# New tokens' value projection in half units between the units of the first attention batches, its product added to the turned attended rows

## The reference

```python
q = jnp.einsum('bsd,ed->bse', x, wq)            # x is the layer norm of the input
k_new = jnp.einsum('bsd,ed->bse', x, wk)
v_new = jnp.einsum('bsd,ed->bse', x, wv)
k = jnp.concatenate([k_cache, k_new], axis=1)   # k_cache = v_cache = the context, 1601 rows
v = jnp.concatenate([v_cache, v_new], axis=1)
scores = jnp.einsum('bqd,bkd->bqk', q, k) * scale
attn = jax.nn.softmax(scores, axis=-1)
out = jnp.einsum('bqk,bkd->bqd', attn, v)       # then out @ wo
```

## Time and profile before

| | |
|---|---|
| median of 3 runs | 1305.7 us (1304.93 to 1308.2) |
| the profiled execution | 1310.41 us |
| its span in the trace | 1308.3 us |
| PE busy | 93% of the span |
| DVE busy, ACT busy | 63%, 48% of the span |
| mean granted TensorE clock | 0.97 |

### The profile page before, as it was taken

How to read it: one execution, slowest core, us unless ns; L and a number is a source line. 1 busy time by engine, 2 the same in 40 slices (tenths; PEclk the granted TensorE clock), 3 DMA queues, 4 the chain that set the end, 5 groups by cost and what they waited for, 6 DMA issues and landing times.

```text
span 1308.3 us, 18916 instructions
## 1 busy us (share of the span) xinstructions
PE 1214.6 (93%) x7634; PEld 1046.4 (80%) x7634; DVE 829.7 (63%) x1013; ACT 628.3 (48%) x562; POOL 97.2 (7%) x82
## 2 busy tenths in 40 slices
PE   4999989888998899999999399999999999999995
PEld 3888766666766688888888398989999999999894
DVE  7332479999999746645546465656556565656464
ACT  4111279888888733113543244444454445454430
POOL 0000100000000000000000011212111111111101
PEclk9999989999998799999999599999999999999998
DMA  7235299999999763421233356676766766676632
GB/s 297 92 129 193 73 360 359 347 388 368 366 356 380 278 267 131 159 97 65 81 123 129 127 184 213 213 213 202 228 212 203 214 218 207 219 209 222 192 128 32
DMA packets 68053, 277.14 MB, mean 212 GB/s; under 512 B 22456, under 2 KB 22600, under 8 KB 45344
## 3 DMA queue, kind: packets, MB, share of 16 engines
q1 hardware_dynamic: 57312, 245.58, 52.3%
q0 software_dynamic: 10688, 30.81, 9.2%
HBM read 258.02 MB, written 18.35 MB: 211 GB/s over the span
## 4 chain that ended last, share of the span: by engine, by line
PE 72%; DVE 13%; DMA 8%; issue 3%; ACT 2%; POOL 0%; SPq 0%; ACTq 0%; DVEq 0%; POOLq 0%
PE ps L1291 22%; PE ps L1292 21%; PE ps L1293 21%; DVE lo L810 10%; DMA out<-y,target 2%; PE ps L1455 2%; DMA raw_more<-new_values 2%; ACT hi L554 1%; PE ps L1387 1%; PE ps L1677 1%; DMA raw<-context 1%; DMA raw<-new_values 1%; DVE scores L888 1%; DMA raw<-keys 1%; PE ps L1406 1%
## 5 line engine op out<-in xcount | busy, mean ns | idle before, releaser
L810 DVE TENSOR_TENSOR lo<-raw,hi 128x2048 fp32r<-128x2048 f32 (+1 forms) x204 | 458.0, 2258 | 173.7 <-ACT hi L554 171.4
L554 ACT ACTIVATE hi<-raw 128x2048 fp32r<-128x2048 f32 (+1 forms) x204 | 383.3, 1888 | 292.8 <-PE ps L1293 270.7
L1291 PE MATMUL ps<-act_hi,hi 128*128 128x240 f32 (+1 forms) x1152 | 333.3, 289 | 9.9 <-DVE act_lo L833 4.8
L1293 PE MATMUL ps<-act_hi,lo 128*128 128x240 f32 (+1 forms) x1152 | 334.2, 290 | 0.0
L1292 PE MATMUL ps<-act_hi,hi 128*128 128x240 f32 x1024 | 283.1, 276 | 0.0
L1291 PEld LDWEIGHTS ps<-act_hi,hi 128*128 128x128 f32 x1152 | 219.0, 190 | 17.7 <-DVE act_lo L833 5.2
L1293 PEld LDWEIGHTS ps<-act_hi,lo 128*128 128x128 f32 x1152 | 219.6, 191 | 5.2
L1292 PEld LDWEIGHTS ps<-act_hi,hi 128*128 128x128 f32 x1024 | 193.8, 189 | 0.3
L1291 PE MATMUL ps<-hi,act_hi 128*128 128x512 f32 x384 | 151.2, 394 | 0.0
L1293 PE MATMUL ps<-hi,act_lo 128*128 128x512 f32 x384 | 149.7, 390 | 0.0
L1292 PE MATMUL ps<-lo,act_hi 128*128 128x512 f32 x384 | 149.5, 389 | 0.0
(11 more groups left out here) (204 smaller groups left out, 1348.0 us busy)
## 6 DMA issues: line engine op xcount, KB each, us to landing
raw<-weights SPq DMA_DIRECT2D x128, 1024.0 KB, 4.9
raw<-keys SPq DMA_DIRECT2D x32, 1024.0 KB, 10.1
raw<-context SPq DMA_DIRECT2D x32, 1024.0 KB, 9.4
raw_more<-keys SPq DMA_DIRECT2D x16, 1024.0 KB, 10.3
raw_more<-context SPq DMA_DIRECT2D x16, 1024.0 KB, 9.7
xq<-x_in SPq DMA_DIRECT2D x4, 512.0 KB, 6.5
new_keys_t<-kvs POOLq DMA_DIRECT2D x8, 256.0 KB, 3.1
new_values<-kvs POOLq DMA_DIRECT2D x8, 256.0 KB, 2.3
```

Of the source, the lines that this page charges most:

```text
L554: act.activation(part(hi, k, kind), part(raw, k, kind), ACT.Copy).then_inc(hi_done, 1)
L810: dve.tensor_tensor(part(lo, k, kind), part(raw, k, kind), part(hi, k, kind), ALU.subtract).then_inc(lo_done, 1)
L1291: pe.matmul(out, a_hi, b_hi, start=first, stop=False)
L1293: return pe.matmul(out, a_lo, b_hi, start=False, stop=last)
```

## The change

The value projection is no longer a stage of its own. Its four units become 8 half units ("block", 128 x 1024), each of which gives 128 dimensions of the new values for all 512 tokens, turned (`value_block`, 24 matmuls of 512 columns). They stand behind unit 2 of the first eight stretches: keys 0, keys 1, values 0, keys 2, values 1, keys 3, values 2, keys 4. ACT copies the block from PSUM (`block_copy`), PE turns it with 4 transposes (`turn_block`), and ACT copies it to `new_v` in SBUF (`new_v_copy`). The stores of the new values to DRAM and their reloads are gone, and the last value unit holds 65 rows of 1024 floats instead of 128 of 2048.

The product with the new values leaves the values stretch (4 matmuls of 512 columns each). The weights of the new tokens are turned by one matmul against an identity that DVE has scaled by the reciprocal of the sum (`turn_new_weights`), and the product is added to the turned attended rows, in float32 with 64 columns: for batches 4 to 7 inside `turn_o` (8 more matmuls), for batches 0 to 3 later, twice in each of values 5 and values 6 (`late`, 16 matmuls each: 8 to bring the kept rows back to PSUM, 8 products).

The scores of the last key unit now lie in PSUM bank 5 behind the turned weights, so PE waits before that unit until these have been split (`pt_split`, `rinv_ready`). ACT writes the low score rows straight into `S`. SP waits for 8 stores, those of the keys, before the first reload.

```diff
+def attention_units():
+    blocks = iter(range(C))
+    def stretch(what, b, extra):
+        for u in range(7):
+            yield what, b, u
+            if u == 2 and extra:
+                yield "block", None, next(blocks)
+    units = list(stretch("keys", 0, True))
+    for s in range(B):
+        if s + 1 < B:
+            units += stretch("keys", s + 1, s < 4)
+        units += stretch("values", s, s < 3)
+    assert next(blocks, None) is None
+    return units
+ATTENTION = attention_units()
...
+            def load_block(k, f):
+                load(k, w_d[W_V + f // 2, :, (f % 2) * D:(f % 2 + 1) * D], dst=raw_of(k)[:, 0:D])
...
-            for n in range(8):
-                g, t = n // TT, n % TT
-                pool.wait_ge(evacuated, O_V + n + 1)
-                pool.dma_start(new_v_d[t * P:(t + 1) * P, g * HALF:(g + 1) * HALF],
-                               kvs[:, n % 2, :]).then_inc(kv_stored[n % 2], 16)
-
...
+        def scores_at(j, rows):
+
+            return ps[rows, j, 0:HALF] if j < 3 else ps[rows, 5, TAIL_AT:TAIL_AT + KTAIL + QL]
...
+            def new_weights(s):
+                rows = rows_of_step(s)
+                act.wait_ge(new_p_ready, s + 1)
+                act.activation(new_p[rows, s // 2, :], ps[rows, NEW_P_BANK, 0:QL], ACT.Copy).then_inc(new_p_copied, 1)
...
+            def turned_copy(s):
+                act.wait_ge(ot_ready, s + 1)
+                view = ps[:, 6, :].rearrange("p (c n) -> p c n", c=C)
+                if s < LATE:
+                    act.wait_ge(q_split, s + 1)
+                    act.activation(q[:, s, :, :], view, ACT.Copy).then_inc(early_copied, 1)
+                else:
+                    act.activation(act_hi[:, :, s * QL:(s + 1) * QL], view, ACT.Copy).then_inc(ot_hi_done, 1)
+            def late(b):
+                act.wait_ge(late_ready, b + 1)
+                act.activation(act_hi[:, :, b * QL:(b + 1) * QL], ps[:, LATE_BANK, :].rearrange("p (c n) -> p c n", c=C),
+                               ACT.Copy).then_inc(late_hi, 1)
+            def block_copy(f):
+                act.wait_ge(block_ready, f + 1)
+                if f > 0:
+                    act.wait_ge(block_turned, f)
+                act.activation(block_t[:, :], ps[:, BLOCK_BANK, :], ACT.Copy).then_inc(block_copied, 1)
+            def new_v_copy(f):
+                act.wait_ge(block_turned, f + 1)
+                act.activation(new_v[:, :, f * P:(f + 1) * P], ps[:, NEW_V_BANK, :].rearrange("p (t n) -> p t n", t=TT),
+                               ACT.Copy).then_inc(new_v_copied, 1)
...
+                dve.wait_ge(rinv_ready, s + 1)
+                dve.tensor_scalar(scaled_ident[rows, :], ident[rows, rows], rinv[rows, s % 2:s % 2 + 1], None,
+                                  ALU.mult).then_inc(scaled_ready, 1)
...
-            projection(U_V, O_V)
...
+                if u == 6 and s > 0:
+                    pe.wait_ge(pt_split, 2 * s)
+                    pe.wait_ge(rinv_ready, s)
...
+            def turn_new_weights(s):
+                rows = rows_of_step(s)
+                pe.wait_ge(scaled_ready, s + 1)
+                pe.wait_ge(pt_split, 2 * s + 2)
+                if s + 1 < B:
+                    pe.wait_ge(s_evac, 4 * (s + 1) + 4)
+                pe.matmul(ps[rows, NEW_P_BANK, 0:QL], S[rows, KV:KEYS], scaled_ident[rows, :],
+                          start=True, stop=True).then_inc(new_p_ready, 1)
+            def turn_o(s):
+                pe.wait_ge(o_norm, s + 1)
+                if s >= LATE:
+                    pe.wait_ge(new_v_copied, C)
+                    pe.wait_ge(new_p_copied, s + 1)
+                rows = rows_of_step(s)
+                for c in range(C):
+                    out = ps[:, 6, c * QL:(c + 1) * QL]
+                    ins = pe.matmul(out, O[:, c * P:(c + 1) * P], twice[:, 0:QL], start=True, stop=(s < LATE))
+                    if s >= LATE:
+                        ins = pe.matmul(out, new_v[rows, s // 2, c * P:(c + 1) * P], new_p[rows, s // 2, :],
+                                        start=False, stop=True)
+                ins.then_inc(ot_ready, 1)
+            def late(b):
+                rows = rows_of_step(b)
+                pe.wait_ge(new_v_copied, C)
+                pe.wait_ge(early_copied, b + 1)
+                pe.wait_ge(new_p_copied, b + 1)
+                pe.wait_ge(block_copied, C)
+                if b > 0:
+                    pe.wait_ge(late_split, b)
+                for c in range(C):
+                    out = ps[:, LATE_BANK, c * QL:(c + 1) * QL]
+                    pe.matmul(out, ident, q[:, b, c, :], start=True, stop=False)
+                    ins = pe.matmul(out, new_v[rows, b // 2, c * P:(c + 1) * P], new_p[rows, b // 2, :],
+                                    start=False, stop=True)
+                ins.then_inc(late_ready, 1)
+            def value_block(f, k):
+                if f == 0:
+                    pe.wait_ge(evacuated, O_QK + 16)
+                else:
+                    pe.wait_ge(block_copied, f)
+                unit_ready(k)
+                for c in range(C):
+                    at = slice(c * P, (c + 1) * P)
+                    ins = three(ps[:, BLOCK_BANK, :], hi[:, k % RING, at], lo[:, k % RING, at],
+                                act_hi[:, c, :], act_lo[:, c, :], c == 0, c == C - 1)
+                ins.then_inc(block_ready, 1)
+            def turn_block(f, s):
+                pe.wait_ge(block_copied, f + 1)
+                if f > 0:
+                    pe.wait_ge(new_v_copied, f)
+                if s >= 0:
+                    pe.wait_ge(pt_split, 2 * s + 1)
+                for t in range(TT):
+                    ins = pe.transpose(ps[:, NEW_V_BANK, t * P:(t + 1) * P], block_t[:, t * P:(t + 1) * P], ident)
+                ins.then_inc(block_turned, 1)
+            def values(s, u, k):
...
+                for j in range(2 if u < 6 else 1):
+                    kc = 2 * u + j
+                    rows = slice(0, P if kc < 12 else KREM)
...
+            def attention():
+                turned_blocks = 0
+                for n, (what, b, u) in enumerate(ATTENTION):
+                    k = U_KEYS0 + n
+                    if what == "block":
+                        value_block(u, k)
+                    elif what == "keys":
+                        s = b - 1
+                        if u == 2 and s > 0:
+                            turn_o(s - 1)
+                        if u == 4 and s >= 0:
+                            if turned_blocks:
+                                pe.wait_ge(new_v_copied, turned_blocks)
+                            turn_weights(s)
+                        score_block(b, u, k)
+                        if u == 6 and s < 0:
+                            turn_block(turned_blocks, s)
+                            turned_blocks += 1
                     else:
-                        ins.then_inc(unit_used, 1)
-
-            for u in range(7):
-                score_block(0, u)
-            step(0)
-            for s in range(1, B - 1):
-                step(s)
-            step(7, nxt=False)
-
-            pe.wait_ge(ot_split, B - 2)
+                        s = b
+                        if u == 0 and s == B - 1:
+                            turn_o(s - 1)
+                            turn_weights(s)
+                        if u in (1, 6) and turned_blocks < blocks_before(n):
+                            turn_block(turned_blocks, s)
+                            turned_blocks += 1
+                        if u == 2:
+                            turn_new_weights(s)
+                        if s in (5, 6) and u in (2, 5):
+                            late(2 * (s - 5) + u // 3)
+                        values(s, u, k)
+                assert turned_blocks == C
```

More of the change, by code:

```diff
@@ L97, in released @@
         unit("out_ready", O_QK + 2 * (k + 1))
[L98 to L105 removed]
+    for what, b, u in ATTENTION:
+        if what == "block":
+            unit("block_ready", u + 1)
+        elif what == "keys":
+            unit(*(("s_ready", 4 * b + (u + 1) // 2 + (u == 6)) if u % 2 or u == 6 else (None, 0)))
+        else:
+            unit(*(("o_ready", b + 1) if u == 6 else (None, 0)))
     by_tile(O_WO)
@@ L849, in _ @@
             dve.tensor_tensor(wr_lo[:, :, :], wr_raw[:, :, :], wr_hi[:, :, :], ALU.subtract).then_inc(wr_split, 1)
-            for k in range(U_Q, U_V):
+            for k in range(U_Q, U_KEYS0):
                 split(k + AHEAD)
@@ new lines, in attention @@
+            def attention():
+                for n, (what, b, u) in enumerate(ATTENTION):
+                    split(U_KEYS0 + n + AHEAD)
+                    if what == "keys":
+                        s = b - 1
+                        if u in (1, 3, 5):
+                            score_add(b, u // 2)
+                        if u == 1 and s > LATE:
+                            turned_lo(s - 1)
+                        if u == 4 and s >= 0:
+                            weights_lo(s)
```

(17 more changed lines are left out.)

478 lines of the change are left out of this document (225 added, 253 removed).

## The result

The changed kernel is slower. Its time is 1340.3 us (median of four runs, 1335.7 to 1341.3) against 1305.3 us for the kernel before on the same chip: a ratio of 1.0255, with a 95% interval from 1.0227 to 1.0282. The forecast was 1289, with 1279 to 1300 as its range.

What follows compares the result with a forecast made beforehand. PE was to bound the first half and DVE's splits to pace the second. 21.3 us gained by the end of values 6, less 4.4 in the tail, made -16.9 from 1305.7: 1289 us, range 1279 to 1300.

Steps and rivals of the forecast that it cites:

- two `late` of 16 x 0.24 = 3.8 each: Second half, PE's own work: each of two values stretches, 19.7 us long, holds two `late` runs of 3.8 us.
- `turn_o` twice as long: Second half, PE's own work: the doubled `turn_o` makes two keys stretches 18.8 us each.
- my 119.0: Second half: PE's own work in us, "just below" the time forecast for the half; also its lower bound.
- the 128.1: Second half to the end of values 6: 131.2 - 4.6 - 1.5 + 3.0 us, the 3.0 for waits before last key units.
- The start: Before the attention: the 43.9 us value projection goes, so PE starts the attention at 117.8 instead of 161.7 us.
- The first half: First score to values 3: PE becomes the bound, 167.4 + 1.7 + 1.2 = 170.3 us; values 3 starts at 288.1, 18.2 earlier.
- The one before the last key unit: First half: PE's new wait for both halves of the split weights, taken as 0.3 us four times, 1.2 in all.
- The half unit of keys 1: First half: a wait of 1.7 us before this half unit, from counting through ACT's queue.
- The tail: After values 6: +4.4 us, from `turn_o(6)` +3.7 at half clock, -1.2 for removed work, and `turn_o(7)` +1.9.
- Slower: Rival, 11%: the wait before the last key unit costs in full in seven keys stretches; 1303 or no gain, up to 1311.
- Loads pace the second half: Rival, 8%: second half's 47.3 MB needs 128.4 us at 368 GB/s or 131.4 at 360, +3.3, kernel 1292 or 1293.
- More is given back: Rival, 22%: waits at half units and transposes (+8) or no lead into the second half (+4.6); about 1294 to 1301.

Runs made afterwards that it cites:

- alternate_full_rows: Changed kernel, same alternating order and sums, but the new values' products use all 128 rows, mixing two batches' shares; 1304.0 us (one run).
- grouped: Changed kernel with the eight 128-row products issued together, then the eight 64-row ones, in `turn_o` (batches 4 to 7) and `late`, sums left out; 1308.2 us.
- tail_own_bank: Changed kernel with the last key unit's scores back in bank 3, waiting for block copies and score evacuation instead of split weights and row sums; 1336.4 us.
- folded: Changed kernel with batches 4 to 7's new values inside the value sum, `late` eight like products added by DVE, last key scores in bank 3; 1292.7 us.
- full_rows_own_bank: Changed kernel with 128-row products of the new values (two batches' shares mixed) and the last key unit's scores in bank 3; 1298.9 us.

## Why the prediction was wrong

**The step that failed** is the price of the new product in the second half: "two `late` of 16 x 0.24 = 3.8 each" and "`turn_o` twice as long". I took the price of a run of like products, 0.236 us, for a run that alternates between 128 and 64 rows. It is 0.36. With the half clock inside the runs the six of the half took 41.7 us and not 22.8: +18.9. At 0.363 throughout, the 96 products would take 34.8, so some 12 us of this are the order and 7 the clock, an estimate. Behind them the ordinary matmuls ran at the half clock, 10.7 us more than in the same six places of alternate_full_rows. So more of the loss is the clock, which my 119.0 took as full, than the price itself. In the second half the two came and went together only in part: with full rows no run lost the clock, but in grouped, at the old price, five of six did. PE's own work there was put at 119.0; with these two it is 148.6, already above the 128.1 at which DVE was to pace the half, and the trace has PE busy for 153.9. The rest, 5.3 us, is partly half clock behind the 2.41 us wait (16 value matmuls in 6.09 instead of some 4.0); I have not divided it further. PE idles for another 7.2, of which 4.4 are the waits before the last key units (2.41, 0.87, 1.13), where 3.0 was the term. That this step is the cause, and not one that looks like it, is shown by the runs: without the products 1287.5, with them at equal rows 1304.0.

**The start** was right: 117.8 forecast, 115.6 measured, 116.2 to 117.8 in the other kernels.

**The first half** was put at 170.3 and took 176.3, so values 3 began at 291.9 and not at 288.1. PE is the bound there, as said: busy 166.5 us against 167.4, DVE at 82% (80 to 85 forecast), clock 0.98. That the busy times agree so well is partly luck: at the full clock, which I had assumed, the same instructions take 162.8 us (tail_own_bank), so my prices were 4.6 us too high and the half clock made up for most of it. Three waits were mis-sized. The one before the last key unit:

```profile
160.13 0.30 PE L1471 MATMUL ps<-hi,qs 128*128 128x130 f32 x1 [1.14 <-DVE rinv L983]
...
203.39 0.30 PE L1471 MATMUL ps<-hi,qs 128*128 128x130 f32 x1 [0.89 <-DVE rinv L983]
...
246.88 0.30 PE L1471 MATMUL ps<-hi,qs 128*128 128x130 f32 x1 [1.14 <-DVE rinv L983]
...
290.11 0.30 PE L1471 MATMUL ps<-hi,qs 128*128 128x130 f32 x1 [0.88 <-DVE rinv L983]
...
324.65 0.30 PE L1471 MATMUL ps<-hi,qs 128*128 128x130 f32 x1 [2.41 <-DVE rinv L983]
```

Four times make 4.05 us, not 1.2. The half unit of keys 1 waited 2.48 us, not 1.7. And the starts of keys 2 to 4 waited about 1.0 us each for their split, which I had at nothing. Together 6.6 us more, about the 6.0 that are missing. In tail_own_bank, where the first of the three is gone, the half is 5.1 us shorter, 1.4 of it by shorter gaps.

**The tail** grew by 4.4 us to the end of values 7, where 2.5 were due by then: `turn_o(6)` took 9.7 us and not 7.3. `turn_o(7)`, put at +1.9, took 7.7 us instead of 1.89, and the first 12 output matmuls behind it ran at the half clock: +8.5 in all. With full rows the same window grew by 1.8 (29.5 against 27.7), which is the term as I had it.

**The rivals.** "Slower" had the right sign and the wrong mechanism: its wait is real, but removing it left the kernel at 1336. It was put down to DVE's `rinv`, not to `pt` as I had said, and lasted 0.9 to 1.1 us in the first half. "Loads pace the second half" had no chance to show in the changed kernel; in folded, where the products are cheap, the half takes 129.5 us at the 368 GB/s from which I had worked out 128.4. "More is given back" happened in the first half. What no rival held was a product dearer than its neighbour of the same number of columns, or a clock that falls while PE is busy. My remark that `late` and `turn_o` fit "just below" should have been the warning: a bound that lies 9 us under the forecast needs its unit price from a row of that very form, and there was none. The 64-row blocks of the kernel before stood in runs of their own (263.53 in the earlier trace rows), and I had no bound from above for the mixture.

## What to carry to other kernels

Price a small matmul by what stands next to it, not by its columns alone: a stream that switches between stationary blocks of 128 and of 64 rows cost 0.36 us per product, where either kind in a run of its own took 0.21 to 0.25. Give both kinds the same height (padding the short block with zeros would do it, which no run here tried), group the kinds, or fold the work into a sum that has no neighbour of the other height. And when work is moved off a stage that has gaps into one that has few, list the unit price of each added instruction with the row that it is from; where the row is of another order or shape, keep the upper end in the range.

## What the hardware showed that I had not expected

- A product of two instructions over 64 columns, from start to start: 0.21 us in a run of 128-row blocks, 0.24 in a run of 64-row blocks, 0.22 when it alternates between two buffers with 128 rows, 0.36 when it alternates between 128 and 64 rows, whether it adds to the sum or starts it.
- The granted clock fell to 1.2 GHz while PE was busy without a gap: 2.2 to 5.4 us into the six alternating runs of the second half, and behind five of the six grouped runs of 3.8 us. It did not fall in or behind the six 3.5 us runs of 128-row products in alternate_full_rows, and with a 512-column matmul behind each pair it fell behind one stretch of six. With a wait of 0.98 or 1.35 us ahead, two of the 128-row runs lost it too (full_rows_own_bank). No run separates which of these differences decides.
- The folded kernel gets PE's 44 us of projection off the path before the attention and keeps some 14 of them (1292.7 against 1307.0), with the loads at 368 GB/s again the limit of the second half.
